# Moving VectorE's waits for the filled inputs to the reduces, and swapping the two waits ahead of the hidden state, in a stack of recurrent layers

## The chip, the cores and the metric

One core of one Trainium2 chip. The metric is the time of one execution in microseconds (us), the median of several runs. An interval for a change comes from runs of both kernels on the same chip.

## What is computed

The input x is 4 sequences of 1024 tokens with 512 features; cond is one vector of 512 per sequence. Four residual layers follow each other:

```
x = x + rnn(x)      # h = tanh(x_t @ Wx + b + h @ Wh), h0 = cond
x = x + ssm(x)      # convolution, softplus and tanh gates, a diagonal linear scan
x = x + lstm(x)     # A = x_t @ Wx + b + h @ Wh; i, f, o = sigmoid, g = tanh
                    # c = f*c + i*g; h = o * tanh(c), h0 = cond, c0 = 0
x = x + adapter(x)  # x @ (base + low-rank matrix made from cond)
```

The RNN and the LSTM are recurrences over 1024 tokens: a step needs the hidden state of the step before. Everything else is matrix products over many tokens at once.

## The kernel before

Time is cut into 32 chunks of 32 tokens, and the layers are pipelined over chunks: while the LSTM works through chunk i-2, the SSM works on chunk i-1 and the RNN on chunk i. Inside a chunk every engine runs through 32 steps `s`. There are 1024 LSTM steps in all (chunks 2 to 33 of the pipeline) and 1024 RNN steps (chunks 0 to 31). Chunks 0 to 3 are written out, the middle ones are a loop that holds two chunks, and the last five are written out again.

One LSTM step. The gates' 16 blocks are two halves, h = 0 and h = 1. TensorE (L1012) waits for `lstm_h_ready0`, issues 24 matmuls, waits for `lstm_h_ready1`, issues 16 more (these 40 finish half 0 and give `lstm_mm0`) and then the last 24 (`lstm_mm1`). Then come the RNN's 32 matmuls (L1051) and, in some steps, work of the other layers, or three filler products on an identity matrix.

VectorE's order in a step is written by hand (L856 to L893). The names in front are used in what follows, with the line of the instruction:

- transpose(0), L732: copies half 0 out of PSUM in 32x32 blocks into `lstm_sums`
- reduce(0), L737: adds the parts of the product and the input part, which GpSimd (L347) has copied into three columns of the same tile beforehand, and gives the gates' argument
- the SSM's piece of vector work (only in steps 3 to 8 of a chunk; a second piece comes after the LSTM's work)
- transpose(1), products(0) (L743: i*g and f*c), reduce(1), new_cell(0) (L748), out_gate(0) (L752)
- transpose_rnn (L844), products(1)
- h_part(0) (L768: the hidden state in float32), hi_part(0) (L771: its float16 part), new_cell(1), lo_part(0) (L775: the float16 rest, gives `lstm_h_ready0`), out_gate(1)
- hi_part(1), h_part(1), reduce_rnn (L849), lo_part(1) (gives `lstm_h_ready1`)
- the RNN's own two operations L890 and L892 (gives `rnn_h_ready`)

ScalarE computes the gates' tanh (L486) after each reduce, the cell's tanh (L491) after each new_cell, and the RNN's tanh (L503). GpSimd refills the input columns two steps ahead (`lstm_in_ready0`, `lstm_in_ready1`, `rnn_x_filled`).

VectorE's own results are guarded with a semaphore too, `vec_done`: reduce waits until its transpose has counted it up, and h_part(0) and hi_part(1) wait for their out_gate. Where the text has two waits in front of one instruction, one of them goes with the instruction, and the other becomes an instruction of its own (EVENT_SEMAPHORE) in front of it. The two waits ahead of the hidden state are `tanh_done`:

```
vec.wait_ge(S["vec_done"], o_at)                # L761
vec.wait_ge(S[f"lstm_tanhc{h}"], s + 1)         # L762
```

Of the kernel before, what the change touches and what calls it, by code (L numbers as in the profile page):

```python
# [16 lines left out]
CT = 32  # L17
# [77 lines left out]
def resid_stack_kernel(nc, x, cond, l0_Wx, l0_Wh, l0_b, conv_b, Wp, bp, Ws, bs, A_log, dt_log, Wo, bo,  # L95
                       l2_Wx, l2_Wh, l2_b, base, w1, b1, w2, b2, ln_g, ln_b, out):
    ctx = ExitStack()
    with ctx:
# [478 lines left out]
        def _(vec):  # L577
# [135 lines left out]
            def body(_i, par, known, w, p):  # L713
                S, S_last = sets[par], sets[1 - par]
                n = [0]

                def mark(ins):

                    n[0] += 1
                    ins.then_inc(S["vec_done"], 1)  # L720
                    return n[0]
# [4 lines left out]
                def transpose(h, s):  # L726
                    if known == 2 and s == 0:
                        vec.wait_ge(lstm_h0_mm, KB)
                    if s == 0:
                        vec.wait_ge(S[f"lstm_in_ready{h}"], 1)  # L730
                    vec.wait_ge(S[f"lstm_mm{h}"], s + 1)
                    return mark(V.transpose(tr[h][s % 2][:, :, 0:QC], psL[h][:, 0:HW].rearrange("p (g c) -> p g c", c=QC)))  # L732

                def reduce(h, s, at):
                    vec.wait_ge(S["vec_done"], at)
                    three = tr[h][s % 2][:, :, :].rearrange("p g (s n) -> p g s n", n=NB)[:, :, 0:XS // NB + 1:LO // NB, :]
                    V.tensor_reduce(arg[h][:, :, :], three.rearrange("p g s n -> p g n s"), AX.X, ALU.add  # L737
                                    ).then_inc(S[f"lstm_summed{h}"], 1)

                def products(h, s):  # L740

                    vec.wait_ge(S[f"lstm_gated{h}"], s + 1)
                    return mark(V.scalar_tensor_tensor(out=prod[h][:, :, :], in0=gate[h][:, 0:2, :], scalar=1.0,  # L743
                                                       in1=gate[h][:, G - 1:G + 1, :], op0=ALU.add, op1=ALU.mult))

                def new_cell(h, at):
                    vec.wait_ge(S["vec_done"], at)
                    V.scalar_tensor_tensor(out=cell[h], in0=prod[h][:, 1, :], scalar=0.5, in1=prod[h][:, 0, :],  # L748
                                           op0=ALU.mult, op1=ALU.add).then_inc(S[f"lstm_cell{h}"], 1)

                def out_gate(h):
                    return mark(V.tensor_scalar(o_s[h][:, :], gate[h][:, 2, :], 1.0, H_SCALE, ALU.add, ALU.mult))  # L752

                def next_x_filled(h, s):

                    if s + 1 < CT:
                        vec.wait_ge(S[f"lstm_in_ready{h}"], s + 2)

                def tanh_done(h, s, o_at):

                    vec.wait_ge(S["vec_done"], o_at)  # L761
                    vec.wait_ge(S[f"lstm_tanhc{h}"], s + 1)  # L762

                o3 = [t[:, :].rearrange("p (b n) -> p b n", b=HB) for t in o_s]
                t3 = [t[:, :].rearrange("p (b n) -> p b n", b=HB) for t in tc]
# [1 line left out]
                def h_part(h, s):  # L767
                    return mark(V.tensor_tensor(half(hl, h)[:, :, s, :], o3[h], t3[h], ALU.mult))  # L768

                def hi_part(h):  # L770
                    return mark(V.tensor_tensor(half(hls, h)[:, :, 0:NB], o3[h], t3[h], ALU.mult))  # L771

                def lo_part(h, s, at):
                    vec.wait_ge(S["vec_done"], at)
                    V.tensor_tensor(half(hls, h)[:, :, LO:LO + NB], half(hl, h)[:, :, s, :], half(hls, h)[:, :, 0:NB], ALU.subtract  # L775
                                    ).then_inc(S[f"lstm_h_ready{h}"], 1)
# [62 lines left out]
                def transpose_rnn(s):  # L839
                    if known == 0 and s == 0:  # L840
                        vec.wait_ge(rnn_h0_mm, 1)
                    vec.wait_ge(S["rnn_x_filled"], s + 1)
                    vec.wait_ge(S["rnn_mm"], s + 1)
                    return mark(V.transpose(tr_r[s % 2][:, :, 0:QC], psR[:, 0:RW].rearrange("p (g c) -> p g c", c=QC)))  # L844

                def reduce_rnn(s, at):
                    vec.wait_ge(S["vec_done"], at)
                    three = tr_r[s % 2][:, :, :].rearrange("p g (s n) -> p g s n", n=NB)[:, :, 0:XS // NB + 1:LO // NB, :]
                    V.tensor_reduce(arg_r[:, :, :], three.rearrange("p g s n -> p g n s"), AX.X, ALU.add).then_inc(S["rnn_summed"], 1)  # L849

                for s in range(CT):
                    if s == ARRIVE_STEP:
                        vec.sem_inc(arrive, 1)
                    if w["mid"] and not w["lstm"]:
                        ssm_stage(s, 0)
                    if w["lstm"]:  # L856
                        at = transpose(0, s)
                        reduce(0, s, at)
                        if w["mid"]:
                            ssm_stage(s, 0)  # L860
                        at = transpose(1, s)
                        p_at = products(0, s)
                        reduce(1, s, at)
                        new_cell(0, p_at)
                        o_at = out_gate(0)
                        if w["rnn"]:
                            r_at = transpose_rnn(s)
                        p_at = products(1, s)
                        tanh_done(0, s, o_at)
                        h_part(0, s)  # L870
                        next_x_filled(0, s)
                        at = hi_part(0)
                        new_cell(1, p_at)
                        lo_part(0, s, at)
                        o_at = out_gate(1)
                        tanh_done(1, s, o_at)
                        hi_part(1)
                        next_x_filled(1, s)
                        at = h_part(1, s)
                        if w["rnn"]:  # L880
                            reduce_rnn(s, r_at)
                        lo_part(1, s, at)
                    elif w["rnn"]:
                        r_at = transpose_rnn(s)
                        reduce_rnn(s, r_at)
                    if w["mid"]:
                        ssm_stage(s, 2)
                    if w["rnn"]:
                        vec.wait_ge(S["rnn_tanh"], s + 1)
                        at = mark(V.tensor_scalar(hrs[:, :, 0:NB], hr[:, :, s, :], R_SCALE, None, ALU.mult))  # L890
                        vec.wait_ge(S["vec_done"], at)
                        V.scalar_tensor_tensor(out=hrs[:, :, LO:LO + NB], in0=hr[:, :, s, :], scalar=R_SCALE, in1=hrs[:, :, 0:NB],  # L892
                                               op0=ALU.mult, op1=ALU.subtract).then_inc(S["rnn_h_ready"], 1)  # L893
                    if known in (0, 1):
                        prepare(CT * known + s)
                next_chunk(vec, "vec")

            pipeline(vec, body)


# [279 lines left out]
```

## Time and profile before

| | |
|---|---|
| median of 3 runs | 4081.14 us (4079.91 to 4082.55) |
| profiled execution, its own time | 4081.14 us |
| its span in the profile | 4079.3 us |
| TensorE busy | 3674.6 us (90%) |
| VectorE busy | 3435.0 us (84%) |
| ScalarE busy | 1391.5 us (34%) |
| GpSimd busy | 781.2 us (19%) |
| chain that ended last | VectorE 57%, TensorE 34%, issue 5%, ScalarE 3% |
| granted TensorE clock, mean | 0.995 |

The chain that ended last is followed back from the last instruction, at each step to what released it. Two engines share it, since they hand the hidden state to each other in every step. A busy share says how long an engine had something in it; instructions overlap on VectorE by a few hundredths of a microsecond, and waits that stand as instructions of their own are not counted as busy.

### The profile page before, as it was taken

To read this page: it belongs to the slowest core of one execution; us is meant where nothing else is said; L and a number is where in the kernel's file an instruction comes from. 1 tells how busy PE (TensorE), PEld (TensorE's weight loads), DVE (VectorE), ACT (ScalarE), POOL (GpSimd) and SP (SyncE) were. 2 spreads that over 40 slices of the span, in tenths; PEclk is the share of its full clock that TensorE was granted. 3 is DMA by queue.
4 is the path that set the end of the run, shared out by engine and by line. 5 is a ranking of instruction groups with operands and counts; after the bars stand their busy time and mean duration, and the time that the engine had idled before them with its cause. 6 is when DMAs were issued, how large, how long until landed. Compare 5 with 4: busy or idle time off the path is not lost.

```text
span 4079.3 us, 257765 instructions
## 1 busy us (share of the span) xinstructions
PE 3674.6 (90%) x110802; PEld 3024.6 (74%) x110802; DVE 3435.0 (84%) x21201; ACT 1391.5 (34%) x6196; POOL 781.2 (19%) x3624
## 2 busy tenths in 40 slices
PE   6889999999999999999999999999999999988875
PEld 4677777777777777777777777777777777777654
DVE  5588888888888888888888888888888888888776
ACT  4233333333333333333333333333333333333221
POOL 0112112222121221211222122121211122112111
PEclk8999999999999999999999999999999999999999
DMA  7100000000000000000000000000000000000000
GB/s 264 47 7 7 10 9 9 7 7 9 9 9 9 9 7 7 9 9 9 9 7 7 9 9 9 9 8 8 7 9 9 9 9 7 7 7 7 6 5 8
DMA packets 19076, 63.05 MB, mean 15 GB/s; under 512 B 3959, under 2 KB 4527, under 8 KB 14915
## 3 DMA queue, kind: packets, MB, share of 16 engines
q1 hardware_dynamic: 17692, 46.67, 3.6%
q8 instruction: 869, 14.24, 1.4%
q14 instruction: 221, 1.80, 0.1%
q10 hardware_dynamic: 294, 0.33, 0.0%
HBM read 38.48 MB, written 8.39 MB: 11 GB/s over the span
## 4 chain that ended last, share of the span: by engine, by line
DVE 57%; PE 34%; issue 5%; ACT 3%; DMA 1%; DVEq 0%; SPq 0%; ACTq 0%; POOL 0%; POOLq 0%
PE ps_lstm L1012 27%; DVE lstm_sums L732 18%; DVE lstm_arg L737 7%; DVE lstm_gates_2c L748 5%; DVE lstm_ig_fc L743 5%; DVE rnn_sums L844 5%; DVE lstm_h_scaled L768 4%; DVE lstm_h_parts L771 3%; DVE lstm_h_parts L775 2%; PE ps_rnn L1051 2%; DVE lstm_o_scaled L752 2%; PE ps_lstm_in_b L1093 2%; PE ps_ssm L1093 1%; ACT lstm_tanh_c L491 1%; DVE rnn_h_parts L890 1%
## 5 line engine op out<-in xcount | busy, mean ns | idle before, releaser
L1012 PE MATMUL ps_lstm<-lstm_Wh_parts,lstm_h_parts 128*20 128x256 f16 x65472 | 1987.3, 273 | 354.0 <-DVE lstm_h_parts L775 343.1
L1012 PEld LDWEIGHTS ps_lstm<-lstm_Wh_parts,lstm_h_parts 128*20 128x20 f16 x65472 | 1487.2, 91 | 829.9 <-DVE lstm_h_parts L775 620.6
L732 DVE STREAM_TRANSPOSE lstm_sums<-ps_lstm 128x256 f32<-128x256 f32 x2048 | 910.0, 444 | 139.2 <-PE ps_lstm L1012 75.3
L486 ACT ACTIVATE lstm_gates_2c<-lstm_arg 128x32 f32<-128x32 f32 x2048 | 469.8, 229 | 1574.4 <-DVE lstm_arg L737 1574.4
L347 POOL COPY lstm_sums<-lstm_in 128x32 f32<-128x32 f32 x2048 | 427.6, 212 | 1728.9 <-DVE lstm_arg L737 1720.5
L1051 PE MATMUL ps_rnn<-rnn_Wh_parts,rnn_h_parts 128*20 128x128 f16 x32736 | 641.0, 220 | 39.5 <-DVE rnn_h_parts L892 37.1
L1051 PEld LDWEIGHTS ps_rnn<-rnn_Wh_parts,rnn_h_parts 128*20 128x20 f16 x32736 | 549.5, 92 | 77.3 <-DVE rnn_h_parts L892 56.4
L491 ACT ACTIVATE lstm_tanh_c<-lstm_gates_2c 128x8 f32<-128x8 f32 x2048 | 410.4, 200 | 485.1 <-DVE lstm_gates_2c L748 485.1
L737 DVE TENSOR_REDUCE lstm_arg<-lstm_sums 128x32 f32<-128x96 f32 x2048 | 538.1, 263 | 35.1
L771 DVE TENSOR_TENSOR lstm_h_parts<-lstm_o_scaled,lstm_tanh_c 128x8 f16<-128x8 f32 x2048 | 334.2, 163 | 147.1 <-ACT lstm_tanh_c L491 4.9
L503 ACT ACTIVATE rnn_h<-rnn_arg 128x16 f32<-128x16 f32 x1024 | 220.8, 216 | 602.0 <-DVE rnn_arg L849 602.0
L890 DVE TENSOR_SCALAR rnn_h_parts<-rnn_h 128x16 f16<-128x16 f32 x1024 | 216.4, 211 | 175.4 <-ACT rnn_h L503 174.4
L743 DVE SCALAR_TENSOR_TENSOR lstm_ig_fc<-lstm_gates_2c 128x16 f32<-128x16 f32 x2048 | 350.7, 171 | 9.1
L844 DVE STREAM_TRANSPOSE rnn_sums<-ps_rnn 128x128 f32<-128x128 f32 x1024 | 316.4, 309 | 35.4 <-PE ps_rnn L1051 33.2
L768 DVE TENSOR_TENSOR lstm_h_scaled<-lstm_o_scaled,lstm_tanh_c 128x8 f32<-128x8 f32 x2048 | 334.1, 163 | 11.1 <-issue 6.0
L775 DVE TENSOR_TENSOR lstm_h_parts<-lstm_h_scaled,lstm_h_parts 128x8 f16<-128x8 f32 x2048 | 339.9, 166 | 2.6 <-DVE lstm_h_scaled L768 0.2
L752 DVE TENSOR_SCALAR lstm_o_scaled<-lstm_gates_2c 128x8 f32<-128x8 f32 x2048 | 336.5, 164 | 0.2
L748 DVE SCALAR_TENSOR_TENSOR lstm_gates_2c<-lstm_ig_fc 128x8 f32<-128x8 f32 x2048 | 322.8, 158 | 2.8 <-DVE lstm_h_parts L771 2.8
L1137 PE MATMUL ps_lstm_in_a<-x,lstm_Wx 128*128 128x128 f32 x2048 | 297.5, 288 | 0.0
L1137 PE MATMUL ps_lstm_in_b<-x,lstm_Wx 128*128 128x128 f32 x2048 | 296.9, 288 | 0.0
L1137 PEld LDWEIGHTS ps_lstm_in_a<-x,lstm_Wx 128*128 128x128 f32 x2048 | 248.6, 191 | 34.9 <-issue 8.5
L1137 PEld LDWEIGHTS ps_lstm_in_b<-x,lstm_Wx 128*128 128x128 f32 x2048 | 248.1, 191 | 29.0 <-issue 1.9
(181 smaller groups left out, 2705.8 us busy)
## 6 DMA issues: line engine op xcount, KB each, us to landing
layer_plus_2I<-in_L_cond_w SPq DMA_DIRECT2D x16, 1024.0 KB, 6.0
out<-out_rows SPq DMA_DIRECT2D x128, 64.0 KB, 1.9
x_rows<-in_x SPq DMA_DIRECT2D x31, 256.0 KB
lstm_Wx<-in_L_cond_Wh SPq DMA_DIRECT2D x1, 4096.0 KB, 16.7
lstm_Wx<-in_L_cond_Wx SPq DMA_DIRECT2D x1, 4096.0 KB, 13.6
layer_plus_2I<-in_L_cond_Wh SPq DMA_DIRECT2D x1, 1024.0 KB, 8.9
rnn_Wx<-in_L_cond_Wx SPq DMA_DIRECT2D x1, 1024.0 KB, 11.2
lstm_in<-in_L_cond_w SPq DMA_DIRECT2D x1, 1024.0 KB, 10.0
```

The lines of the kernel that those rows point to most:

```text
L486: A.activation(gate[h][:, 0:G, :].rearrange("p g q -> p (g q)"), arg[h][:, :, :].rearrange("p g n -> p (g n)"), ACT.Tanh, scale=gate_scale ...
L491: A.activation(tc[h][:, :], cell[h], ACT.Tanh, scale=0.5).then_inc(S[f"lstm_tanhc{h}"], 1)
L732: return mark(V.transpose(tr[h][s % 2][:, :, 0:QC], psL[h][:, 0:HW].rearrange("p (g c) -> p g c", c=QC)))
L737: V.tensor_reduce(arg[h][:, :, :], three.rearrange("p g s n -> p g n s"), AX.X, ALU.add).then_inc(S[f"lstm_summed{h}"], 1)
L743: return mark(V.scalar_tensor_tensor(out=prod[h][:, :, :], in0=gate[h][:, 0:2, :], scalar=1.0, in1=gate[h][:, G - 1:G + 1, :], op0=ALU.add ...
L748: V.scalar_tensor_tensor(out=cell[h], in0=prod[h][:, 1, :], scalar=0.5, in1=prod[h][:, 0, :], op0=ALU.mult, op1=ALU.add).then_inc(S[f"lstm ...
L768: return mark(V.tensor_tensor(half(hl, h)[:, :, s, :], o3[h], t3[h], ALU.mult))
L771: return mark(V.tensor_tensor(half(hls, h)[:, :, 0:NB], o3[h], t3[h], ALU.mult))
L844: return mark(V.transpose(tr_r[s % 2][:, :, 0:QC], psR[:, 0:RW].rearrange("p (g c) -> p g c", c=QC)))
L1012: ins = mm(psL[h][QC * j:QC * j + LO + NB, 0:HW], hls[:, k, :], whl[:, k, h, e, j, :], start=(k == 0 and e == 0), stop=(k == KB - 1 and e ...
L1051: last = mm(psR[QC * j:QC * j + LO + NB, 0:RW], hrs[:, k, :], whr[:, k, e, j, :], start=(k == 0 and e == 0), stop=(k == KB - 1 and e == 1) ...
L1137: last = mm(psI[b % 2][:, TOK * b:TOK * (b + 1)], w_, x2[:, k, :, :].rearrange("p t n -> p (t n)"), start=(k == 0), stop=(k == KB - 1))
```

## The change

The wait for the filled input columns goes from three places (the first transpose of a chunk, and one of the two hidden-state operations of each half, where it looked one step ahead) to the reduce that reads the columns. The RNN's goes from its transpose to its reduce. In `tanh_done` the two waits change places. No operation on data is added, removed or moved.

```
--- before.py
+++ after.py
@@ -726,12 +726,11 @@
                 def transpose(h, s):
                     if known == 2 and s == 0:
                         vec.wait_ge(lstm_h0_mm, KB)
-                    if s == 0:
-                        vec.wait_ge(S[f"lstm_in_ready{h}"], 1)
                     vec.wait_ge(S[f"lstm_mm{h}"], s + 1)
                     return mark(V.transpose(tr[h][s % 2][:, :, 0:QC], psL[h][:, 0:HW].rearrange("p (g c) -> p g c", c=QC)))
 
                 def reduce(h, s, at):
+                    vec.wait_ge(S[f"lstm_in_ready{h}"], s + 1)
                     vec.wait_ge(S["vec_done"], at)
                     three = tr[h][s % 2][:, :, :].rearrange("p g (s n) -> p g s n", n=NB)[:, :, 0:XS // NB + 1:LO // NB, :]
                     V.tensor_reduce(arg[h][:, :, :], three.rearrange("p g s n -> p g n s"), AX.X, ALU.add
@@ -751,15 +750,10 @@
                 def out_gate(h):
                     return mark(V.tensor_scalar(o_s[h][:, :], gate[h][:, 2, :], 1.0, H_SCALE, ALU.add, ALU.mult))
 
-                def next_x_filled(h, s):
-
-                    if s + 1 < CT:
-                        vec.wait_ge(S[f"lstm_in_ready{h}"], s + 2)
-
                 def tanh_done(h, s, o_at):
 
+                    vec.wait_ge(S[f"lstm_tanhc{h}"], s + 1)
                     vec.wait_ge(S["vec_done"], o_at)
-                    vec.wait_ge(S[f"lstm_tanhc{h}"], s + 1)
 
                 o3 = [t[:, :].rearrange("p (b n) -> p b n", b=HB) for t in o_s]
                 t3 = [t[:, :].rearrange("p (b n) -> p b n", b=HB) for t in tc]
@@ -839,11 +833,11 @@
                 def transpose_rnn(s):
                     if known == 0 and s == 0:
                         vec.wait_ge(rnn_h0_mm, 1)
-                    vec.wait_ge(S["rnn_x_filled"], s + 1)
                     vec.wait_ge(S["rnn_mm"], s + 1)
                     return mark(V.transpose(tr_r[s % 2][:, :, 0:QC], psR[:, 0:RW].rearrange("p (g c) -> p g c", c=QC)))
 
                 def reduce_rnn(s, at):
+                    vec.wait_ge(S["rnn_x_filled"], s + 1)
                     vec.wait_ge(S["vec_done"], at)
                     three = tr_r[s % 2][:, :, :].rearrange("p g (s n) -> p g s n", n=NB)[:, :, 0:XS // NB + 1:LO // NB, :]
                     V.tensor_reduce(arg_r[:, :, :], three.rearrange("p g s n -> p g n s"), AX.X, ALU.add).then_inc(S["rnn_summed"], 1)
@@ -868,14 +862,12 @@
                         p_at = products(1, s)
                         tanh_done(0, s, o_at)
                         h_part(0, s)
-                        next_x_filled(0, s)
                         at = hi_part(0)
                         new_cell(1, p_at)
                         lo_part(0, s, at)
                         o_at = out_gate(1)
                         tanh_done(1, s, o_at)
                         hi_part(1)
-                        next_x_filled(1, s)
                         at = h_part(1, s)
                         if w["rnn"]:
                             reduce_rnn(s, r_at)
```

## Rows read from the trace of the kernel before

**Rows 1.** The page, part 4: shares of the chain that ended last, by line.
```profile
PE ps_lstm L1012 27%; DVE lstm_sums L732 18%; DVE lstm_arg L737 7%; DVE lstm_gates_2c L748 5%; DVE lstm_ig_fc L743 5%; DVE rnn_sums L844 5%; DVE lstm_h_scaled L768 4%; DVE lstm_h_parts L771 3%; DVE lstm_h_parts L775 2%; PE ps_rnn L1051 2%; DVE lstm_o_scaled L752 2%; PE ps_lstm_in_b L1093 2%; PE ps_ssm L1093 1%; ACT lstm_tanh_c L491 1%; DVE rnn_h_parts L890 1%
```

**Rows 2.** The first transpose's line, all steps: nanoseconds min/median/max, first and last start.
```profile
L732 DVE STREAM_TRANSPOSE lstm_sums<-ps_lstm x2048: 383/443/452, 197.7 to 4066.3; 128x256 f32<-128x256 f32 x187
```

**Rows 3.** Timeline, one plain step: start, duration, engine, line, operation.
```profile
2000.15 0.45 DVE L732 STREAM_TRANSPOSE lstm_sums<-ps_lstm 128x256 f32<-128x256 f32 x1
...
2000.63 0.26 DVE L737 TENSOR_REDUCE lstm_arg<-lstm_sums 128x32 f32<-128x96 f32 x1
2000.81 0.44 DVE L732 STREAM_TRANSPOSE lstm_sums<-ps_lstm 128x256 f32<-128x256 f32 x1
...
2001.29 0.26 DVE L737 TENSOR_REDUCE lstm_arg<-lstm_sums 128x32 f32<-128x96 f32 x1
...
2001.58 0.23 ACT L486 ACTIVATE lstm_gates_2c<-lstm_arg 128x32 f32<-128x32 f32 x1 [0.43 <-DVE lstm_arg L737]
...
2001.72 0.19 ACT L491 ACTIVATE lstm_tanh_c<-lstm_gates_2c 128x8 f32<-128x8 f32 x1
2001.85 0.17 DVE L743 SCALAR_TENSOR_TENSOR lstm_ig_fc<-lstm_gates_2c 128x16 f32<-128x16 f32 x1
2002.01 0.17 DVE L768 TENSOR_TENSOR lstm_h_scaled<-lstm_o_scaled,lstm_tanh_c 128x8 f32<-128x8 f32 x1
...
2002.29 0.17 DVE L775 TENSOR_TENSOR lstm_h_parts<-lstm_h_scaled,lstm_h_parts 128x8 f16<-128x8 f32 x1
2002.37 0.21 ACT L491 ACTIVATE lstm_tanh_c<-lstm_gates_2c 128x8 f32<-128x8 f32 x1 [0.46 <-DVE lstm_gates_2c L748]
2002.38 0.16 DVE L752 TENSOR_SCALAR lstm_o_scaled<-lstm_gates_2c 128x8 f32<-128x8 f32 x1
...
2002.51 1.61 PE L1012 MATMUL ps_lstm<-lstm_Wh_parts,lstm_h_parts 128*20 128x256 f16 x52 [0.45 <-DVE lstm_h_parts L775]
2002.68 0.17 DVE L771 TENSOR_TENSOR lstm_h_parts<-lstm_o_scaled,lstm_tanh_c 128x8 f16<-128x8 f32 x1
...
2002.96 0.17 DVE L775 TENSOR_TENSOR lstm_h_parts<-lstm_h_scaled,lstm_h_parts 128x8 f16<-128x8 f32 x1
...
2003.65 0.18 DVE L892 SCALAR_TENSOR_TENSOR rnn_h_parts<-rnn_h,rnn_h_parts 128x16 f16<-128x16 f32 x1
2003.85 0.45 DVE L732 STREAM_TRANSPOSE lstm_sums<-ps_lstm 128x256 f32<-128x256 f32 x1
```

**Rows 4.** Waits that stand in VectorE's queue as instructions, by line.
```profile
L762 DVEq EVENT_SEMAPHORE  x2048: 21/21/21, 199.5 to 4068.1; - x187
...
L843 DVEq EVENT_SEMAPHORE  x1024: 21/21/745, 19.1 to 3824.9; - x171
...
L731 DVEq EVENT_SEMAPHORE  x64: 21/21/50, 197.0 to 3950.8; - x64
...
L817 DVEq EVENT_SEMAPHORE  x32: 21/21/21, 139.7 to 3862.2; - x32
```

**Rows 5.** The chain of waits in the same step, around the second tanh.
```profile
2002.61 0.02 DVEq L762
```

**Rows 6.** Timeline, the turn from one chunk to the next.
```profile
2009.91 1.83 PE L1012 MATMUL ps_lstm<-lstm_Wh_parts,lstm_h_parts 128*20 128x256 f16 x60 [0.45 <-DVE lstm_h_parts L775]
...
2011.32 0.45 DVE L732 STREAM_TRANSPOSE lstm_sums<-ps_lstm 128x256 f32<-128x256 f32 x1
```

**Rows 7.** Timeline, a step in which TensorE did not go idle.
```profile
2017.53 1.60 PE L1012 MATMUL ps_lstm<-lstm_Wh_parts,lstm_h_parts 128*20 128x256 f16 x52
```

**Rows 8.** Timeline of VectorE, a step with the SSM's last stage.
```profile
2045.56 0.17 DVE L775 TENSOR_TENSOR lstm_h_parts<-lstm_h_scaled,lstm_h_parts 128x8 f16<-128x8 f32 x1
2045.64 0.16 DVE L818 COPY state<-stage 128x2 f32<-128x2 f32 x1
...
2046.55 0.18 DVE L892 SCALAR_TENSOR_TENSOR rnn_h_parts<-rnn_h,rnn_h_parts 128x16 f16<-128x16 f32 x1
2046.64 0.44 DVE L732 STREAM_TRANSPOSE lstm_sums<-ps_lstm 128x256 f32<-128x256 f32 x1
```

More of the change, by code:

```diff
@@ L728, in transpose @@
                         vec.wait_ge(lstm_h0_mm, KB)
-                    if s == 0:
-                        vec.wait_ge(S[f"lstm_in_ready{h}"], 1)
                     vec.wait_ge(S[f"lstm_mm{h}"], s + 1)
@@ L734, in reduce @@
                 def reduce(h, s, at):
+                    vec.wait_ge(S[f"lstm_in_ready{h}"], s + 1)
                     vec.wait_ge(S["vec_done"], at)
@@ L752, in out_gate @@
                     return mark(V.tensor_scalar(o_s[h][:, :], gate[h][:, 2, :], 1.0, H_SCALE, ALU.add, ALU.mult))
-                def next_x_filled(h, s):
-                    if s + 1 < CT:
-                        vec.wait_ge(S[f"lstm_in_ready{h}"], s + 2)
                 def tanh_done(h, s, o_at):
+                    vec.wait_ge(S[f"lstm_tanhc{h}"], s + 1)
                     vec.wait_ge(S["vec_done"], o_at)
-                    vec.wait_ge(S[f"lstm_tanhc{h}"], s + 1)
                 o3 = [t[:, :].rearrange("p (b n) -> p b n", b=HB) for t in o_s]
@@ L841, in transpose_rnn @@
                         vec.wait_ge(rnn_h0_mm, 1)
-                    vec.wait_ge(S["rnn_x_filled"], s + 1)
                     vec.wait_ge(S["rnn_mm"], s + 1)
@@ L846, in reduce_rnn @@
                 def reduce_rnn(s, at):
+                    vec.wait_ge(S["rnn_x_filled"], s + 1)
                     vec.wait_ge(S["vec_done"], at)
@@ L870, in body @@
                         h_part(0, s)
-                        next_x_filled(0, s)
                         at = hi_part(0)
@@ L877, in body @@
                         hi_part(1)
-                        next_x_filled(1, s)
                         at = h_part(1, s)
```

## The prediction

> **What bounds the kernel now.** The page comes first. VectorE and TensorE are both 84 to 90% busy, and neither share decides, since the two hand the hidden state back and forth in each LSTM step. The chain's lines say which way the step closes: TensorE's recurrent product L1012 has 27% of the span [rows 1], 1101 us. The timeline of one step shows why [rows 3]. lo_part(0) starts at 2002.29 and ends at 2002.46; TensorE starts 0.05 later, at 2002.51; transpose(0) of the next step starts at 2003.85, 1.34 after that. VectorE could have begun it sooner: its last operation, L892, started at 2003.65, and back to back the two lie 0.09 apart [rows 8], so 2003.74 was possible. The step is a ring: transpose(0), the two reduces, the gates, lo_part(0), 40 matmuls, the next transpose(0). It takes 2003.85 - 2000.15 = 3.70. All steps on average take (4066.3 - 0.7 - 197.7)/1023 = 3.78 (0.7 lies between the two halves' transposes) [rows 2, 3]. A delay ahead of lo_part(0) is paid in nearly every step.
>
> TensorE has a second wait, for `lstm_h_ready1`, behind 24 matmuls. A matmul takes (1.83 - 1.61)/8 = 0.0275, from the row with 60 of them and the one with 52 [rows 3, 6], so 24 need 0.66, and TensorE gets there at 2003.17. lo_part(1) ends at 2002.96 + 0.17 = 2003.13, and with the same 0.05 it is 2003.18. So half 1 is late by 0.01 already, and half 0 has that much slack.
>
> **What a wait costs, by where it stands.** This change moves no operation, only waits, so the price is the difference between a wait that goes with its instruction and one that stands in the queue alone. Which of two is which is read from the groups of standing waits [rows 4]: L762 has 2048, and L761 none; L843 (RNN product) has 1024, L842 (input filled) none; L731 (LSTM product, first step of a chunk) has 64, the wait before it none. Three times the wait written first stays with the instruction, and the later one stands alone. It isn't the semaphore that decides: the one kept is VectorE's own at L761, GpSimd's in the other two.
>
> With the instruction: transpose(0) ends at 2000.15 + 0.45 = 2000.60, reduce(0) starts at 2000.63, so 0.03. ScalarE's gates end at 2001.58 + 0.23 = 2001.81, and products(1) starts at 2001.85, 0.04 [rows 3]. Alone: the second tanh ends at 2002.37 + 0.21 = 2002.58, the standing wait runs at 2002.61 [rows 5], hi_part(1) starts at 2002.68, so 0.10. The first tanh ends at 2001.91 and h_part(0) starts at 2002.01, again 0.10 [rows 3]. A standing wait that is the last thing to come true costs 0.07 more. The turn of a chunk agrees: there transpose(0) has a standing wait on the product, and starts 1.41 after TensorE's start instead of 1.34 [rows 6].
>
> **The change part by part, in a plain step.** Times are those of [rows 3].
>
> reduce(0) and reduce(1): the input wait now comes first and is kept, true long before. `vec_done` is second and stands alone, and its transpose is the very instruction in front. reduce(0) starts 0.07 later, and transpose(1), 0.18 behind its start, moves with it. transpose(1)'s end plus 0.10 instead of 0.04 makes reduce(1) start 0.14 late. Both reduces stand in the ring. Queued behind the first are transpose(1) and products(0), behind the second new_cell(0), out_gate(0), transpose_rnn and products(1); all move by what their reduce moves. ScalarE's second gates (2001.58) move by 0.14, and the first cell's tanh, which starts 0.14 behind those gates, moves too: it ends at 2002.05.
>
> tanh_done(0): now the tanh is kept with h_part(0), and `vec_done` of out_gate(0) stands alone, true 0.1 and more before. h_part(0) starts at 2002.05 + 0.03 = 2002.08 instead of 2002.01, 0.07 late: the 0.14 less a gain of 0.07. products(1) moves to 1.99, far enough ahead that it doesn't hold h_part(0). hi_part(0), new_cell(1) and lo_part(0) follow, 0.07 late. TensorE starts 0.07 late and then waits 0.01 less for half 1: the ring grows by 0.06.
>
> tanh_done(1): out_gate(1) moves to 2002.45 and ends at 2002.61; its standing wait lets hi_part(1) start at 2002.71. The tanh alone would have allowed 2002.65 + 0.03 = 2002.68. So half 1 is 0.03 late, less than half 0, and lo_part(1) doesn't set the end. The RNN's tail also moves by 0.03: L892 to 2003.68, plus 0.09 is 2003.77, ahead of the new transpose(0) at 2003.91.
>
> transpose_rnn loses its standing wait and reduce_rnn gains one; both are true long before, and TensorE and the reduce have other work ahead. Cost: nothing if VectorE's queue is filled ahead of the engine. Behind L775 the SSM's copy has such a wait (L817) and still starts 0.08 after it, the spacing of its neighbours [rows 4, 8]. In reduce_rnn the wait comes sooner after a stopped queue, so I keep an upper bound of another 0.07 on lo_part(1). The dropped waits at hi_part(0) and h_part(1) were true: they give nothing.
>
> **Per chunk.** Four kinds of steps:
> - Plain: 25 of 32, 0.06 each, 1.50.
> - TensorE full: at the first three steps it has no idle time before L1012 [rows 7] (the SSM's matmuls), and starts about 0.06 after it could. That absorbs all but about 0.01: 3 x 0.01 = 0.03.
> - VectorE full: after steps 4, 5 and 8 transpose(0) follows L892 by 0.09 [rows 8]. They grow by the tail's shift, 3 x 0.03 = 0.09.
> - The turn: transpose(0) has one wait left, so it gains 0.07 against 0.06: -0.01.
>
> The sum is 1.61 a chunk. The LSTM has 32 chunks: 51.5 us. The two chunks in which the RNN runs alone have one standing wait fewer at the transpose and one more at the reduce, 0. The profiled execution took 4081.14 us, the same as the median: 4081.1 + 51.5 = 4133 us, +1.3%.
>
> **Where the price could differ.** No row shows a standing wait on `vec_done` that comes true last. Its lower end is 0, the upper the whole 0.10. At 0.05 instead of 0.07 the ring grows by about 0.03, hardly 25 us; at 0.10 by about 0.12, about 100 us. I take 0.07, since the two standing waits on ScalarE and the one on TensorE agree on it, and the kept waits cost 0.03 to 0.04 on VectorE's own semaphore and on ScalarE's alike.
>
> The Trainium skill speaks against this (VectorE: DVE Perf Modes, the section on the DRAIN you can't avoid): a row of vector operations took the same time with a semaphore after each as with one after the last, and "the semaphore costs nothing extra here". By that rule the waits at the reduces would be free, and the sum would be that of the first rival.
>
> **Rivals.**
> - *Faster: waits on VectorE's own semaphore cost 0 extra.* Then the reduces stay, and only the tanh waits gain. h_part(0) starts at 2001.91 + 0.03, 0.07 early; out_gate(1) ends at 2002.47, hi_part(1) may start at 2002.50, held by the tanh to 2002.54, over 0.1 early. The ring shrinks by 0.07 in plain steps, by up to 0.14 in the VectorE-full ones, with the turn another 0.07: 25 x 0.07 + 3 x 0.12 + 0.14 = 2.25 a chunk at most, 72 us, and 58 if the TensorE wait for half 1 and the spacing behind products(1) take a fifth. 4023 us. For it: nothing but the sameness of a DVE-to-DVE and an ACT-to-DVE wait when kept is known. Against: reduce(0) is issued right behind its transpose, so the wait can't be true early, and standing waits need 0.10 in all places seen. It decides from a price below about 0.035, where two reduces no longer outweigh one tanh. 7%.
> - *Much slower: half 1 becomes the late one.* The standing wait in reduce_rnn comes two instructions after a stopped queue and adds its 0.07 to L849 and lo_part(1): 0.03 + 0.07 = 0.10 late, and 0.10 in plain and VectorE-full steps. 28 x 0.10 + 0.10 = 2.9 a chunk, 93 us, about 4170. Against: the copy behind L817 [rows 4, 8]. 13%.
> - *No change: which wait stands alone is decided otherwise,* so that `vec_done` is kept at the reduces and the tanh stands alone as before. Only the turn gains: 32 x 0.07 = 2 us, 4079. Against: three times the first one kept [rows 4]. 3%.
> - *Slower, by a quarter to a half of it,* because price or slack is smaller than the rows' hundredths say: 4095 to 4110. 7%.
>
> **Numbers.** Likeliest, 70%: 4133, own range 4115 to 4150. Faster by over 0.2% (8 us, about what a measurement here can tell from no change) 0.07, within it 0.03, slower 0.90. The range reaches from part of the smaller case to the much slower one: 4103 to 4172.
>
> **What the profile after would show.** Standing waits: 2048 at reduce's wait for `vec_done`, 1024 at reduce_rnn's, 2048 at the `vec_done` line of tanh_done, none at transpose_rnn's, none at the chunk's first transpose. From transpose(0) to reduce(0) 0.55 instead of 0.48. From the tanh's end to h_part(0) 0.03 instead of 0.10. transpose(0) to lo_part(0) 2.21 instead of 2.14. A plain step of 3.76. From lo_part(1)'s end to the 25th matmul no wait. Wrong if reduce(0) stays at 0.48, or if lo_part(1) moves by more than 0.06. TensorE's granted clock should stay at 0.99: its idle time grows by 0.06 in 3.7.

## The result, and the profile after

The changed kernel is slower: 4140.14 us (median of 4 runs, 4138.58 to 4149.03) beside 4080.52 us for the kernel before (4 runs, 4068.61 to 4082.55). The ratio is 1.0156, with a 95% interval of 1.0133 to 1.0181. The profiled execution took 4143.03 us.

The page of the changed kernel: span, busy times, the chain by engine and by line.

```profile
span 4141.2 us, 259756 instructions
...
PE 3671.7 (89%) x110802; PEld 3049.4 (74%) x110802; DVE 3429.5 (83%) x21201; ACT 1392.3 (34%) x6196; POOL 781.3 (19%) x3624
...
DVE 56%; PE 35%; issue 6%; ACT 1%; DVEq 1%; DMA 1%; SPq 0%; ACTq 0%; POOL 0%; POOLq 0%
PE ps_lstm L1004 28%; DVE lstm_sums L730 18%; DVE lstm_arg L736 11%; DVE rnn_sums L837 5%; DVE lstm_h_scaled L762 4%; DVE lstm_gates_2c L747 3%; DVE lstm_h_parts L769 3%; DVE lstm_h_parts L765 2%; DVE lstm_o_scaled L751 2%; PE ps_rnn L1043 2%; DVE lstm_ig_fc L742 2%; PE ps_lstm_in_b L1085 2%; PE ps_ssm L1085 1%; DVE rnn_h_parts L882 1%; DVE rnn_h_parts L884 1%
```

TensorE and VectorE have the busy time they had, to 6 us, and the span is 62 us longer. So the added time is waiting and not work, and TensorE's granted clock has no part in it (0.993, 0.995 before). TensorE's recurrent product is still the closing piece of the ring, 28% of the chain (it was 27% [rows 1]). The reduce, L736, was 7% of the chain and is 11% now.

The timeline of one plain step after the change, with the columns of [rows 3].

```profile
2032.69 0.45 DVE L730 STREAM_TRANSPOSE lstm_sums<-ps_lstm 128x256 f32<-128x256 f32 x1
...
2033.25 0.26 DVE L736 TENSOR_REDUCE lstm_arg<-lstm_sums 128x32 f32<-128x96 f32 x1
2033.43 0.44 DVE L730 STREAM_TRANSPOSE lstm_sums<-ps_lstm 128x256 f32<-128x256 f32 x1
...
2033.97 0.26 DVE L736 TENSOR_REDUCE lstm_arg<-lstm_sums 128x32 f32<-128x96 f32 x1
...
2034.40 0.19 ACT L491 ACTIVATE lstm_tanh_c<-lstm_gates_2c 128x8 f32<-128x8 f32 x1
2034.53 0.17 DVE L742 SCALAR_TENSOR_TENSOR lstm_ig_fc<-lstm_gates_2c 128x16 f32<-128x16 f32 x1
2034.62 0.17 DVE L762 TENSOR_TENSOR lstm_h_scaled<-lstm_o_scaled,lstm_tanh_c 128x8 f32<-128x8 f32 x1
...
2034.90 0.17 DVE L769 TENSOR_TENSOR lstm_h_parts<-lstm_h_scaled,lstm_h_parts 128x8 f16<-128x8 f32 x1
2034.98 0.21 ACT L491 ACTIVATE lstm_tanh_c<-lstm_gates_2c 128x8 f32<-128x8 f32 x1 [0.39 <-DVE lstm_gates_2c L747]
2034.99 0.16 DVE L751 TENSOR_SCALAR lstm_o_scaled<-lstm_gates_2c 128x8 f32<-128x8 f32 x1
...
2035.12 1.60 PE L1004 MATMUL ps_lstm<-lstm_Wh_parts,lstm_h_parts 128*20 128x256 f16 x52 [0.52 <-DVE lstm_h_parts L769]
2035.25 0.17 DVE L765 TENSOR_TENSOR lstm_h_parts<-lstm_o_scaled,lstm_tanh_c 128x8 f16<-128x8 f32 x1
...
2035.53 0.17 DVE L769 TENSOR_TENSOR lstm_h_parts<-lstm_h_scaled,lstm_h_parts 128x8 f16<-128x8 f32 x1
...
2036.10 0.17 DVE L884 SCALAR_TENSOR_TENSOR rnn_h_parts<-rnn_h,rnn_h_parts 128x16 f16<-128x16 f32 x1
2036.45 0.45 DVE L730 STREAM_TRANSPOSE lstm_sums<-ps_lstm 128x256 f32<-128x256 f32 x1 [0.17 <-PE ps_lstm L1004]
```

Transpose(0) starts at 2032.69 and its reduce at 2033.25, 0.56 later, where it was 0.48 (counted from the transpose's end, 0.103 where it was 0.034, each the middle value of 1024 steps); the second reduce is 1.28 behind transpose(0) (1.14 before), and lo_part(0) 2.21 (2.14 before). The first tanh ends at 2034.40 + 0.19 = 2034.59, and h_part(0) starts 0.03 behind it (0.10 before; over all steps the middle values are 0.033 and 0.102). out_gate(1) ends at 2034.99 + 0.16 = 2035.15, and hi_part(1) starts 0.10 behind that: there the standing wait for VectorE's own semaphore is the last one. The next transpose(0) comes 3.76 after the first (3.70 before).

The waits that stand alone in VectorE's queue, by line.

```profile
L734 DVEq EVENT_SEMAPHORE  x2048: 21/21/21, 200.3 to 4129.8; - x187
...
L756 DVEq EVENT_SEMAPHORE  x2048: 21/21/21, 201.7 to 4131.1; - x187
...
L841 DVEq EVENT_SEMAPHORE  x1024: 21/21/21, 21.5 to 3882.6; - x171
...
L836 DVEq EVENT_SEMAPHORE  x5: 21/21/21, 19.4 to 123.1; - x5
```

L734 is the reduces' wait for `vec_done`, L756 the one in `tanh_done`, L841 the one in reduce_rnn. At transpose_rnn, L836, five are left in the first 123 us.

### The profile page after: what moved, and what is told of

Read it like the earlier page. It is cut to its first block, busy times and chain, and to the rows that moved or that the text cites. A ratio compares the mean times of both kernels' runs of the same rounds, so it can differ in the third digit from the quotient of the medians.

```text
span 4141.2 us, 259756 instructions
## 1 busy us (share of the span) xinstructions
PE 3671.7 (89%) x110802; PEld 3049.4 (74%) x110802; DVE 3429.5 (83%) x21201; ACT 1392.3 (34%) x6196; POOL 781.3 (19%) x3624
## 4 chain that ended last, share of the span: by engine, by line
DVE 56%; PE 35%; issue 6%; ACT 1%; DVEq 1%; DMA 1%; SPq 0%; ACTq 0%; POOL 0%; POOLq 0%
PE ps_lstm L1004 28%; DVE lstm_sums L730 18%; DVE lstm_arg L736 11%; DVE rnn_sums L837 5%; DVE lstm_h_scaled L762 4%; DVE lstm_gates_2c L747 3%; DVE lstm_h_parts L769 3%; DVE lstm_h_parts L765 2%; DVE lstm_o_scaled L751 2%; PE ps_rnn L1043 2%; DVE lstm_ig_fc L742 2%; PE ps_lstm_in_b L1085 2%; PE ps_ssm L1085 1%; DVE rnn_h_parts L882 1%; DVE rnn_h_parts L884 1%
## 5 line engine op out<-in xcount | busy, mean ns | idle before, releaser
L1004 PEld LDWEIGHTS ps_lstm<-lstm_Wh_parts,lstm_h_parts 128*20 128x20 f16 x65472 | 1509.8, 91 | 868.0 <-DVE lstm_h_parts L769 687.9
L736 DVE TENSOR_REDUCE lstm_arg<-lstm_sums 128x32 f32<-128x96 f32 x2048 | 537.7, 263 | 115.7 <-DVE lstm_ig_fc L742 0.7
```

The costliest lines, as they stand in the source:

```text
L1004: ins = mm(psL[h][QC * j:QC * j + LO + NB, 0:HW], hls[:, k, :], whl[:, k, h, e, j, :], start=(k == 0 and e == 0), stop=(k == KB - 1 and e ...
```

## The experiments

Three theories are told apart. A, that of the prediction: a wait that stands alone costs 0.07 us more than one that goes with its instruction, where it is the last thing to come true, and nothing elsewhere. B: each wait that stands alone has one price, wherever it is. C: waits on VectorE's own semaphore are free, and the time comes from elsewhere in the change. Each run has its own runs of the kernel before beside it, and the ratio is against those.

### The reduces' part alone

The changed kernel, with the old order in `tanh_done`:

```
-                    vec.wait_ge(S[f"lstm_tanhc{h}"], s + 1)
                     vec.wait_ge(S["vec_done"], o_at)
+                    vec.wait_ge(S[f"lstm_tanhc{h}"], s + 1)
```

> The change without the swap in tanh_done: the tanh wait stands alone again. Theory A (a standing wait costs 0.07 us where it is the last to come true): reduce(0) 0.07 and reduce(1) 0.14 late as in the changed kernel, no gain at the tanhs, so lo_part(0) and lo_part(1) both 0.14 late, 2.28 us from transpose(0) to lo_part(0), a plain step 3.84, and 4081 + 32 x (28 x 0.14 + 3 x 0.08 + 0.07) = 4216, with 10 for the longer instruction stream 4226 us. Theory B (each wait that stands alone has one price, wherever it is): five standing waits a step as in the changed kernel, so its time, 4140. Theory C (waits on VectorE's own semaphore are free and the time came from the swap): as the kernel before, 4081.

Measured: 4216.57 us (4213.02 to 4217.68), ratio 1.0351 (1.0334 to 1.0368). Transpose(0), lo_part(0) and the next transpose(0) of a plain step:

```profile
2053.16 0.45 DVE L730 STREAM_TRANSPOSE lstm_sums<-ps_lstm 128x256 f32<-128x256 f32 x1
...
2055.44 0.17 DVE L769 TENSOR_TENSOR lstm_h_parts<-lstm_h_scaled,lstm_h_parts 128x8 f16<-128x8 f32 x1
...
2056.99 0.45 DVE L730 STREAM_TRANSPOSE lstm_sums<-ps_lstm 128x256 f32<-128x256 f32 x1
```

lo_part(0) is 2.28 behind transpose(0), and the step takes 3.83, as theory A had it to 0.01. B and C fall. Without the swap the change costs more than twice as much.

### The swap alone

The kernel before, with this edit:

```
+                    vec.wait_ge(S[f"lstm_tanhc{h}"], s + 1)
                     vec.wait_ge(S["vec_done"], o_at)
-                    vec.wait_ge(S[f"lstm_tanhc{h}"], s + 1)
```

> The kernel before with only the two waits of tanh_done swapped. Theory A: h_part(0) 0.07 early; out_gate(1)'s standing wait lets hi_part(1) start 0.11 early; TensorE no longer waits for half 1, which gives another 0.01. Plain step 3.62, VectorE-full ones 0.11 shorter, TensorE-full ones as before: 4081 - 32 x (26 x 0.08 + 3 x 0.11) = 4004 us; 4012 if the spacing behind products(1) holds h_part(0) for 0.01. Theory B: three standing waits as before, 4081. Theory C: the swap is what cost the time, 4140.

Measured: 3998.26 us (3994.80 to 4000.70), ratio 0.9818 (0.9802 to 0.9835). The timeline of a plain step whose transpose(0) starts at 2029.94:

```profile
2029.94 0.45 DVE L732 STREAM_TRANSPOSE lstm_sums<-ps_lstm 128x256 f32<-128x256 f32 x1 [0.17 <-PE ps_lstm L1012]
...
2031.52 0.19 ACT L491 ACTIVATE lstm_tanh_c<-lstm_gates_2c 128x8 f32<-128x8 f32 x1
...
2031.74 0.17 DVE L768 TENSOR_TENSOR lstm_h_scaled<-lstm_o_scaled,lstm_tanh_c 128x8 f32<-128x8 f32 x1
...
2032.02 0.17 DVE L775 TENSOR_TENSOR lstm_h_parts<-lstm_h_scaled,lstm_h_parts 128x8 f16<-128x8 f32 x1
...
2032.65 0.17 DVE L775 TENSOR_TENSOR lstm_h_parts<-lstm_h_scaled,lstm_h_parts 128x8 f16<-128x8 f32 x1
...
2033.56 0.45 DVE L732 STREAM_TRANSPOSE lstm_sums<-ps_lstm 128x256 f32<-128x256 f32 x1
```

The first tanh ends at 2031.52 + 0.19 = 2031.71 and h_part(0) starts at 2031.74, so 0.03; lo_part(0) is 2.08 behind transpose(0), lo_part(1) 2.71, where it was 2.14 and 2.81 [rows 3]. The next transpose(0) starts at 2033.56, a step of 3.62, which is what theory A gave.

### The changed kernel with its own wait written first

In all three reduces (the RNN's has `rnn_x_filled` for its input):

```
+                    vec.wait_ge(S["vec_done"], at)
                     vec.wait_ge(S[f"lstm_in_ready{h}"], s + 1)
-                    vec.wait_ge(S["vec_done"], at)
```

> The changed kernel with the wait for vec_done written first in the three reduces, so that it goes with the instruction and the one for the filled inputs stands alone, true long before. The number of standing waits and of instructions is the changed kernel's. Theory A: reduce(0) back at 0.48 behind transpose(0), the ring as with the swap alone, and the turn 0.07 shorter: 4002, with 10 for the longer instruction stream 4012 us. Theory B: 4140. If the move of the input waits to the reduces were what costs (a late fill): 4140 too, with a late reduce that names GpSimd.

Measured: 4004.58 us (4000.45 to 4008.32), ratio 0.9834 (0.9817 to 0.9850). Transpose(0), its reduce, lo_part(0) and the next transpose(0) of a plain step:

```profile
2032.26 0.45 DVE L730 STREAM_TRANSPOSE lstm_sums<-ps_lstm 128x256 f32<-128x256 f32 x1 [0.16 <-PE ps_lstm L1004]
...
2032.74 0.26 DVE L736 TENSOR_REDUCE lstm_arg<-lstm_sums 128x32 f32<-128x96 f32 x1
...
2034.33 0.17 DVE L769 TENSOR_TENSOR lstm_h_parts<-lstm_h_scaled,lstm_h_parts 128x8 f16<-128x8 f32 x1
...
2035.88 0.45 DVE L730 STREAM_TRANSPOSE lstm_sums<-ps_lstm 128x256 f32<-128x256 f32 x1
```

The reduce is back at 0.48. This kernel has as many standing waits and instructions as the changed one, and its input waits are where the changed one has them. Its ratio is 0.9834 where the changed kernel's is 1.0156, 3.2% or about 131 us, by the order of two lines ahead of the three reduces. So neither the number of waits nor the place of the input waits made the loss.

### VectorE's own wait alone, no input wait moved

The kernel before, with a wait that is already true there (transpose has waited for the same) written ahead of the reduce's own:

```
                 def reduce(h, s, at):
+                    vec.wait_ge(S[f"lstm_mm{h}"], s + 1)
                     vec.wait_ge(S["vec_done"], at)
```

> The kernel before with one edit: each LSTM reduce gets a second wait, always true, written first (its half's matmuls, which its transpose has waited for already), so that the wait for vec_done stands alone. No input wait is moved, tanh_done is as before. Theory A (the 0.07 us belong to the standing wait that comes true last, not to the moved input waits): the ring of the reduces-only run, whose median was 4216.6, without its gain of 0.07 at the turn: 4219. If the moved waits had a part in it: clearly under 4200.

Measured: 4225.30 us (4224.42 to 4231.80), ratio 1.0354 (1.0338 to 1.0370). The reduces-only run had the ratio 1.0351. A step from its transpose(0) to the next, with its two reduces and lo_part(0):

```profile
2079.23 0.45 DVE L732 STREAM_TRANSPOSE lstm_sums<-ps_lstm 128x256 f32<-128x256 f32 x1
...
2079.78 0.26 DVE L738 TENSOR_REDUCE lstm_arg<-lstm_sums 128x32 f32<-128x96 f32 x1
...
2080.50 0.26 DVE L738 TENSOR_REDUCE lstm_arg<-lstm_sums 128x32 f32<-128x96 f32 x1
...
2081.51 0.17 DVE L776 TENSOR_TENSOR lstm_h_parts<-lstm_h_scaled,lstm_h_parts 128x8 f16<-128x8 f32 x1
...
2083.06 0.45 DVE L732 STREAM_TRANSPOSE lstm_sums<-ps_lstm 128x256 f32<-128x256 f32 x1
```

The reduces stand 0.55 and 1.27 behind transpose(0), lo_part(0) 2.28, where it was 2.14: 0.14 more ahead of lo_part(0), 0.07 for each reduce. The step takes 3.83, 0.13 more than in [rows 3]; over the plain steps the middle value went from 3.700 to 3.837. A semaphore of VectorE's own has the same price as ScalarE's. The one instruction more for each reduce is not what costs: the first kernel of "More standing waits that are always true", below, adds as many elsewhere.

### The RNN's part alone

```
                 def transpose_rnn(s):
-                    vec.wait_ge(S["rnn_x_filled"], s + 1)
                     vec.wait_ge(S["rnn_mm"], s + 1)
...
                 def reduce_rnn(s, at):
+                    vec.wait_ge(S["rnn_x_filled"], s + 1)
                     vec.wait_ge(S["vec_done"], at)
```

> The kernel before with only the RNN's wait for its input moved from transpose_rnn to reduce_rnn, where vec_done then stands alone. Theory A: the wait is true long before, and the standing one at the transpose is gone: 4075, within 0.1%. The rival of the prediction (half 1 becomes the late one, by 0.07 a step through reduce_rnn): lo_part(1) 0.07 later, and since TensorE already waits 0.01 for it, 4075 + 28 x 32 x 0.07 = 4138.

Measured: 4085.45 us (10 runs, 4080.88 to 4088.60), ratio 1.0007 (0.9997 to 1.0016): no difference. Transpose(0), lo_part(0), reduce_rnn, lo_part(1) and the next transpose(0):

```profile
2003.87 0.45 DVE L732 STREAM_TRANSPOSE lstm_sums<-ps_lstm 128x256 f32<-128x256 f32 x1
...
2006.02 0.17 DVE L775 TENSOR_TENSOR lstm_h_parts<-lstm_h_scaled,lstm_h_parts 128x8 f16<-128x8 f32 x1
...
2006.57 0.20 DVE L849 TENSOR_REDUCE rnn_arg<-rnn_sums 128x16 f32<-128x48 f32 x1
2006.69 0.17 DVE L775 TENSOR_TENSOR lstm_h_parts<-lstm_h_scaled,lstm_h_parts 128x8 f16<-128x8 f32 x1
...
2007.58 0.45 DVE L732 STREAM_TRANSPOSE lstm_sums<-ps_lstm 128x256 f32<-128x256 f32 x1
```

lo_part(1) starts 2.82 behind transpose(0), beside 2.81 in [rows 3] (over the plain steps the middle values are the same, 2.81). The standing wait in reduce_rnn, two instructions behind a stopped queue, costs nothing, and the prediction's "much slower" rival is gone.

### More standing waits that are always true

The kernel before, in front of the gates' products:

```
                     vec.wait_ge(S[f"lstm_gated{h}"], s + 1)
+                    vec.wait_ge(S[f"lstm_mm{h}"], s + 1)
```

> The kernel before with two more standing waits a step that are always true (the gates' products wait for their matmuls once more), 25 instructions in VectorE's queue per step instead of 23, as in the changed kernel. Theory A with the instruction stream: no plain step changes (3.70), but the stalls of 0.3 us at fixed places of the loop, which stand 4 to a pass of two chunks in the kernel before and 8 in the changed one, grow by about 10 us in all: 4091 us. Theory B: two more standing waits cost what the changed kernel's two do, 4140. If the stalls have nothing to do with the number of instructions: 4081.

Measured: 4080.77 us (10 runs, 4076.00 to 4084.78), ratio 1.0011 (1.0002 to 1.0021), 4 to 6 us where 10 were expected. A plain step takes 3.70, as before. Then the same with five such waits for each half. In the trace of that kernel the line has 6144 standing instructions, six a step, since one holds up to two waits:

```
+                    for _ in range(5):
+                        vec.wait_ge(S[f"lstm_mm{h}"], s + 1)
```

> The kernel before with six more standing instructions per step that are always true, in front of the gates' products (29 instead of 23 in VectorE's queue). Theory A with the instruction stream: two of them gave about 5 us, so six give 10 to 20 and no plain step changes: 4090. Theory B: three times the 60 us that two more had: 4260. If the stream has nothing to do with the rest of the time: 4075.

Measured: 4089.47 us (10 runs, 4083.90 to 4095.12), ratio 1.0018 (1.0009 to 1.0028), some 7 us. A standing wait that is already true costs hardly anything: six instructions a step give 0.007 us a step. Two gave 4 to 6 us and six 7, so the cost isn't shown to be proportional to the number. Theory B, which had 4260, is out by far.

### The version that follows

The swap alone (not shown again), the product wait written first at the turn, and in steps with LSTM work the RNN's input wait placed on out_gate(0), which had no wait:

```
                         vec.wait_ge(lstm_h0_mm, KB)
+                    vec.wait_ge(S[f"lstm_mm{h}"], s + 1)
                     if s == 0:
                         vec.wait_ge(S[f"lstm_in_ready{h}"], 1)
-                    vec.wait_ge(S[f"lstm_mm{h}"], s + 1)
...
-                    vec.wait_ge(S["rnn_x_filled"], s + 1)
+                    if not w["lstm"]:
+                        vec.wait_ge(S["rnn_x_filled"], s + 1)
...
+                        if w["rnn"]:
+                            vec.wait_ge(S["rnn_x_filled"], s + 1)
                         o_at = out_gate(0)
```

> The swap alone, and two more edits: in steps with LSTM work the wait for the RNN's filled input is placed on out_gate(0), which had none, so transpose_rnn keeps its product wait and nothing stands alone there; and at the turn of a chunk the product wait is written first. Theory A: the RNN's part is off the ring, the turn gives 32 x 0.07 = 2 us, and one instruction less per step about 2 us: 3994 beside 3998 of the swap alone. Theory B (a price per standing wait, about 30 us for one per step): 3970.

Measured: 3995.49 us (5 runs, 3992.51 to 4000.13), ratio 0.9788 (0.9774 to 0.9801). It is faster than the kernel before and than the changed one. Against the swap alone (0.9818) the intervals just fail to meet, but that one ran on another occasion, against its own runs of the kernel before, whose medians differ by 8 us (4074.82 and 4082.90); whether the two small edits give anything of their own stays open.

## Why the prediction was right

**Which wait stands alone.** As read from the groups: first written, kept. The standing waits after are the 2048, 1024 and 2048 that were named, and none at the chunk's transpose, but for the two halves of the very first LSTM step, which have a wait for h0 in front.

**The price, 0.07.** Right, at all four places of the step shown: reduce(0) 0.07 late, reduce(1) 0.14 late, h_part(0) 0.03 behind the tanh instead of 0.10, hi_part(1) 0.10 behind out_gate(1). This was the open term, since no row of before had a standing wait on `vec_done` that came true last; the run with VectorE's own wait alone settled it: two of them make lo_part(0) 0.14 late. What makes a standing wait slower by 0.07 no run shows.

The Trainium skill's rule (VectorE: DVE Perf Modes, the DRAIN you can't avoid), by which a semaphore costs nothing extra, does not hold here for a wait that stands alone and is the last to come true: the trace has 0.10 from the end of one operation to the start of the next, where a kept wait has 0.03. The measurement decides.

**The sum in a plain step.** lo_part(0) came 0.07 late as forecast, and half 1 by 0.03 (lo_part(1) 2.84 behind transpose(0), beside 2.81). The forecast for the step was 3.76; over all plain steps the middle one took 3.755, where it had been 3.700. TensorE's wait for half 1 went as forecast too: its 25th matmul started 0.05 behind lo_part(1)'s end before, and starts 0.08 behind it after (middle values), so it no longer waits there.

**The sum of a chunk.** To part it, the distances between one transpose(0) and the next were sorted by their position in the chunk, and the 20th percentile of each position taken for all its steps. The sum over the 1023 distances is 3823.5 us before and 3871.7 us after: 48 us, where the prediction had 51.5. The plain steps' 0.055 instead of 0.06 takes off 25 x 0.005 x 32 = 4 us. The three steps full on VectorE grew by 0.03 each and the turn shrank by 0.02, as forecast to 0.01. Of the three taken as full on TensorE, two absorb the delay (0.01 each) and the first does not: it grew by 0.055 like a plain one, 1 us in all.

**What it missed.** The rest of the distances, what single steps have above that percentile, is 44.4 us before and 57.0 us after. A good part of it is stalls at fixed places of the loop, once in each pass. One of them after the change: ScalarE's tanh, and VectorE's products(1) and h_part(0).

```profile
2107.41 0.19 ACT L491 ACTIVATE lstm_tanh_c<-lstm_gates_2c 128x8 f32<-128x8 f32 x1
2107.54 0.17 DVE L742 SCALAR_TENSOR_TENSOR lstm_ig_fc<-lstm_gates_2c 128x16 f32<-128x16 f32 x1
2107.98 0.17 DVE L762 TENSOR_TENSOR lstm_h_scaled<-lstm_o_scaled,lstm_tanh_c 128x8 f32<-128x8 f32 x1 [0.26 <-DVE lstm_ig_fc L742]
```

The tanh ended at 2107.60 and out_gate(0) long before, yet h_part(0) started at 2107.98, 0.38 later, instead of 0.03. The step took 4.09 (2105.71 to 2109.80). Before, stalls of 0.2 to 0.4 us in nearly every pass stood at four places of the loop's 64 steps besides the turn (steps 26, 37, 42 and 53 of a pass, 17 us together); after, at six (14, 24, 29, 39, 49 and 54, 25 us together), with smaller ones of 0.1 at two more (19 and 44, 3 us together). The distances are multiples of 5.5 steps and then of 5, and VectorE's queue has 23 and then 25 instructions a step: both make 125 to 127 instructions. The transfer of instructions on one queue, q14, grows with them. Before, after, and with six true waits:

```profile
q14 instruction: 221, 1.80, 0.1%
```

```profile
q14 instruction: 235, 1.93, 0.2%
```

```profile
q14 instruction: 267, 2.19, 0.2%
```

Its packets have 8 KB, which is what 1.80 MB in 221 of them gives. Before, one starts in 202 of the 1023 steps, and in every one of the 53 stalled steps at the four places; after, in all but two of the 107 at the eight places. At most of these places it starts 0.7 us behind the late instruction. Most of the other steps with a packet, over 130 of 147 before, have no such stall. The same queue from 2105 to 2110, around the stall shown:

```profile
q14 instruction: 1, 0.01, 0.4%
```

The reading is that VectorE runs out of instructions where a new block of its stream has to come in at a bad moment. The position, the count and the packets speak for it; no run shows it directly. The runs with true waits, 4 to 7 us, show that some of it comes with the number of instructions, but not in proportion. The 12.6 us by which the rest grew are those of two profiled executions, and such sums scatter: the other kernels with 25 instructions a step have 48.0 to 54.0, and those with 23 have 41.0 (the swap alone) and 50.7 (the RNN's part alone). The stalls at the fixed places grew by 10 us. So the match of forecast (4133) and profiled execution (4143) hides two things: 3 us too many in the ring, and 5 to 13 us left out. What is left over between the two profiled executions is 1 us: 2 us more ahead of the first LSTM step (its transpose started at 199.9 instead of 197.7, [rows 2]) and 1 us less behind the last. The other kernels' first transposes lie between 193.9 and 198.5 without order, so that is left as scatter.

**The turn.** The transpose has no standing wait there any more. TensorE's start and transpose(0) of the first step of a chunk:

```profile
2038.87 1.70 PE L1004 MATMUL ps_lstm<-lstm_Wh_parts,lstm_h_parts 128*20 128x256 f16 x53 [0.51 <-DVE lstm_h_parts L769]
...
2040.20 0.45 DVE L730 STREAM_TRANSPOSE lstm_sums<-ps_lstm 128x256 f32<-128x256 f32 x1
```

It starts 1.33 behind TensorE, beside 1.41 in [rows 6]: the gain of 0.07 is there (with the 0.01 that every step gains here), 2 us in all.

**The rivals.** The faster one (own waits free) and the unchanged one (another rule for which wait stands alone) fall with the rows after; the much slower one with the RNN's part alone, and the smaller loss (4095 to 4110) with the measured 4140. The faster rival's other half was right, though: the swap by itself gives 1.8%.

## What to carry to other kernels

Where an instruction has two waits, place the one that comes true last so that it goes with the instruction (in this program, the one written first), and let the early one stand alone; here the order of two lines ahead of three reduces was worth 3.2%, about 131 us. Look in the profile which wait stands alone before relying on the order. Count the waits on a ring that closes in every step, since 0.07 us there is 2% of a step, and don't count those that are true early. A wait can also be put on a neighbour that has none, and then nothing has to stand alone; what that gives by itself stayed open here.

## What the runs showed that was not expected

- One standing instruction takes up to two waits: five extra waits made three instructions, 29 a step instead of 23.
- A standing wait that is true early is free even two instructions behind a stopped queue (reduce_rnn: 1.0007, 0.9997 to 1.0016), and six more instructions a step cost 0.18% (0.09 to 0.28).
- TensorE's start to the next transpose(0) went from 1.34 to 1.33 in the step shown (middle values 1.334 and 1.323), once half 1 was no longer the late one: that is the 0.01 by which the prediction had half 1 late.
- The stalls of 0.2 to 0.4 us at fixed places of the loop, and that they move when VectorE's queue gets longer.
